# The row maxima of both units of a burst taken in a row, in an attention and mixture-of-experts kernel

## The reference

```python
def xattn(x, context, w_q, w_k, w_v, w_o, b_o):      # 16 heads of 64
    q, k, v = heads(x @ w_q), heads(context @ w_k), heads(context @ w_v)
    attn = softmax(q @ k.T * 64 ** -0.5)
    return merge(attn @ v) @ w_o + b_o

def ffn(x, gate, W1, b1, W2, b2):                    # 8 experts, the best 2 of each token
    raw = softmax(x @ gate)
    w = normalised(top_2(raw))
    return sum_e(w[e] * (relu(x @ W1[e] + b1[e]) @ W2[e] + b2[e]))

x = x + xattn(layernorm(x), ctx, ...)
x = x + ffn(layernorm(x), ...)
```

## Time and profile before

| | |
|---|---|
| median of 3 runs | 1580.39 us (1580.01 to 1581.38) |
| the profiled execution: own time, span | 1580.22 us, 1578.5 us |
| TensorE (PE) busy | 1553.8 us, 98% |
| VectorE (DVE) busy | 1176.1 us, 75% |
| ScalarE (ACT) busy | 1108.0 us, 70% |
| GpSimd (POOL) busy | 818.1 us, 52% |

### The profile page before, as it was taken

One profiled execution on the slowest core, in us unless ns is written; L12 is line 12 of the kernel. 1 busy time (PEld: TensorE's weight loads), 2 busy tenths in 40 slices (PEclk: granted clock), 3 DMA queues, 4 the chain that ended last, 5 costly groups with the idle time before them and its releaser, 6 DMA issues.

```text
span 1578.5 us, 45424 instructions
## 1 busy us (share of the span) xinstructions
PE 1553.8 (98%) x14150; PEld 1454.0 (92%) x14151; DVE 1176.1 (75%) x3796; ACT 1108.0 (70%) x3357; POOL 818.1 (52%) x946
## 2 busy tenths in 40 slices
PE   8999999999999999999999999999999999999997
PEld 7899999999899999999999989998899999999997
DVE  4777777777777777777777777777788777777775
ACT  5677677677776777767767777676666676777774
POOL 2344545545554554554555455455456555555556
PEclk9999999999999999999999999999999999999999
DMA  6522111222111221211122211122799755555554
GB/s 201 145 72 74 60 60 60 77 90 72 62 60 60 67 94 66 74 60 60 63 75 89 74 60 60 60 67 81 241 231 249 144 86 85 89 86 90 84 84 61
DMA packets 105643, 145.05 MB, mean 92 GB/s; under 512 B 12736, under 2 KB 87616, under 8 KB 105344
## 3 DMA queue, kind: packets, MB, share of 16 engines
q1 hardware_dynamic: 60144, 89.00, 17.8%
q0 software_dynamic: 26816, 37.32, 13.7%
q10 hardware_dynamic: 18640, 18.19, 4.4%
HBM read 77.09 MB, written 67.38 MB: 92 GB/s over the span
## 4 chain that ended last, share of the span: by engine, by line
issue 47%; POOL 22%; PE 9%; DVE 7%; DMA 6%; DVEq 3%; ACT 2%; POOLq 2%; ACTq 1%; SPq 0%
POOL lists L662 7%; DMA out<-stage_room,number 6%; PE bank_a L1404 4%; POOL prob L669 3%; DVE hid L1332 3%; POOL rstd L648 2%; DVE stage_room L1349 2%; POOL stage_room L711 2%; POOL stage_room L707 2%; POOL out L735 2%; DVEq L1344 1%; PE bank_v L1437 1%; POOLq L729 1%; PE bank_s L1422 1%; DVEq L1323 1%
## 5 line engine op out<-in xcount | busy, mean ns | idle before, releaser
L669 POOL TENSOR_TENSOR prob<-prob,inv 128x512 f32<-128x512 f32 x256 | 271.4, 1060 | 520.3 <-DVE inv L956 519.6
L777 ACT ACTIVATE prob<-bank_s,low 128x128 f32<-128x128 f32 x1024 | 363.3, 376 | 40.9 <-DVE low L951 40.9
L735 POOL DMA_INDIRECT out<-stage_room,number x142 | 231.8, 1632 | 53.9 <-issue 53.1
L951 DVE TENSOR_REDUCE low<-bank_s 128x4 f32<-128x512 f32 x256 | 175.4, 685 | 98.0 <-PE bank_s L1422 97.9
L777 ACT ACTIVATION_READ_ACCUMULATOR prob<-bank_s,low 128x1 f32 x1024 | 221.1, 216 | 0.0
L770 ACT ACTIVATE probt<-bank_t 128x512 f32<-128x512 f32 x256 | 153.4, 599 | 89.6 <-PE bank_t L1411 89.6
L1050 DVE SCALAR_TENSOR_TENSOR stage_room<-xin,wo_t 128x256 f32<-128x256 f32 x480 | 178.8, 426 | 0.0
L807 ACT ACTIVATE ot_h<-bank_v 128x512 fp32r<-128x512 f32 x128 | 77.4, 604 | 138.4 <-PE bank_v L1437 138.4
L885 ACT ACTIVATE hidt_h<-hid 128x512 fp32r<-128x512 f32 x142 | 89.7, 632 | 117.4 <-DVE hid L1332 112.2
L1411 PE MATMUL bank_t<-ident,prob 128*128 128x128 f32 x1024 | 161.9, 281 | 4.0 <-POOL prob L669 4.0
L1404 PE MATMUL bank_a<-xt_l,wq_h 128*128 128x256 f32 x512 | 152.4, 298 | 0.3 <-DVE xt_l L966 0.3
(11 more groups left out here) (231 smaller groups left out, 4728.9 us busy)
## 6 DMA issues: line engine op xcount, KB each, us to landing
stage_room<-lists ACTq DMA_DIRECT2D x67, 265.0 KB
halves<-stage_room SPq DMA_DIRECT2D x32, 512.0 KB
homes<-halves SPq DMA_DIRECT2D x16, 1024.0 KB, 6.4
xin<-in_x SPq DMA_DIRECT2D x32, 256.0 KB, 2.8
stage_room<-in_x SPq DMA_DIRECT2D x32, 256.0 KB
stage_room<-in_w SPq DMA_DIRECT2D x32, 256.0 KB, 4.3
out<-stage_room SPq DMA_DIRECT2D x32, 256.0 KB, 2.2
cin<-in_ctx SPq DMA_DIRECT2D x32, 128.0 KB, 2.6
```

What stands on the lines that cost most here:

```text
L669: pool.tensor_tensor(prob[:, n % 4, :, :], prob[:, n % 4, :, :], wide(inv[:, n % 4, :], P), ALU.mult).then_inc(s_norm.sem, 1)
L735: pool.indirect_dma_start(out, bass.IndirectOffsetOnAxis(ap=number[:, u, b:b + 1], axis=0), ysum[:, u, b, :], None, compute_op=ALU.add).th ...
L777: e = act.activation(prob[:, n % 4, h, :], bank_s[n % 2][:, h * P:(h + 1) * P], ACT.Exp, bias=low[:, n % 4, h:h + 1], scale=-1.0, accum_ou ...
L951: dve.tensor_reduce(low[:, n % 4, :], bank_s[n % 2][:, :].rearrange("p (h k) -> p h k", h=4), AX.X, ALU.min).then_inc(s_low.sem, 1)
```

## The change

VectorE takes the extremes of both units in the even slot, one right behind the other, and nothing in the odd slot. ScalarE makes the exponentials of u0 and u1 of pass 0 back to back in slot 0; in all other places its order stays.

```diff
--- before.py
+++ after.py
@@ -816,7 +816,11 @@
                             copy_t(it, late, (n - 2) % 8)
                         if n == 6 and has(it, PREV):
                             numerators(it, x1[:, :, D:])
-                        if has(it, CUR):
+                        if isinstance(it, int) and it == 0 and n < 2:
+                            if n == 0:
+                                exps(it, 0)
+                                exps(it, 1)
+                        elif has(it, CUR):
                             exps(it, n)
                         for name, o in A_SLOTS[n]:
                             if (name, o) in HI_EVENTS and has(it, o):
@@ -1122,8 +1126,9 @@
                     for n in range(8):
                         if isinstance(it, int) and (it, n) in WHEN:
                             prepare(*WHEN[it, n])
-                        if has(it, CUR):
+                        if n % 2 == 0 and has(it, CUR):
                             lowest(it, n)
+                            lowest(it, n + 1)
                         if n == 1 and has(it, NEXT):
                             wait(dve, ln1_step, it, "bn1_1")
                         if n == 4 and has(it, PREV):
```

## The result

The changed kernel took **1600.08 us** (median of 4 runs, 1599.09 to 1601.43) against 1580.57 for the kernel before: ratio 1.0123, 95% interval 1.0108 to 1.0138. It is slower by 19.5 us where 4.4 were forecast, and outside the range of 1581.2 to 1587.4.

A forecast was written before the change was run, and what follows sets the result against it. The prediction took TensorE, busy in 98% of the span, to bound the kernel; in the loop it never waits for VectorE or ScalarE. Its terms, 4.4 - 0.6 + 0.6 = +4.4 us, gave 1584.8 us, range 1581.2 to 1587.4.

The forecast's parts named there:

- I take these at nothing: Loop slots other than slot 4's chain: shifts of 0.60 us have room, so no cost; otherwise up to 0.1 us a pass.
- Term 1: Loop, passes 1 to 30: new TensorE wait before k00 for the context's low part, 30 x 0.145 = +4.4 us.
- the edge needs 0.11 and has 0.11: Slot 4: from the low part's end to k00's weight load there is no room, so 0.14 to 0.15 us a pass.
- The lower bound: Loop at k00: 30 x 0.08 = +2.4 us, if the edge needs only 0.05 as that from GpSimd does.
- the wait at k00 swallows that of u3's transposition: Slot 4's chain: u3's transposition, 0.08 us late, need not be counted apart, as a later wait on VectorE's line covers it.
- A larger wait: Rival, loop: u3's transposition over 0.1 us late, or reduction costing 0.69: 0.25 us a pass, +7.5, 1588 us; chance 0.06.
- Term 2: Pass 0: TensorE's second burst 1.22 us sooner, its wait 0.96, then a chain in slot 4 longer by 0.60: -0.6 us.
- the bound of -1.2: Pass 0: the gain in us if the longer chain in slot 4 doesn't bind.
- Term 3: Last pass: TensorE's waits for u3 and u5 come 0.60 later without adding up: +0.6 us, bounds 0 and +1.5.
- The edge has room: Rival, loop at k00: the low part is wanted later or VectorE has slack, loop at zero, 1580.4 us; chance 0.14.
- the ends pay: Rival, pass 0: the whole 2.18 us wait and the lower-clock stretch go, the loop doesn't pay, 1576.5 us; chance 0.06.
- The clock: Rival, loop: new short waits bring TensorE to half its clock once a pass, +28 us, 1613 us; chance 0.02.

The follow-up runs named there:

- B: Session on one chip: one-slot versions of the change against the kernel before, pass 0 only 0.9990, pair in slot 2 only 1.0005, reciprocal between slot 2's reductions 1.0014.
- E: Session on one chip, single executions: changed kernel 1597.79 us; slot 4 paired with transfers 0.6 later 1597.54; changed kernel with fourth transfer moved away 1583.02.
- slot 4 alone: Against the kernel before, VectorE's two reductions paired in slot 4 only, in every pass, ScalarE's order as before: 1582.45 us, ratio 1.0010.
- chip A: Chip of the first measurement and traces, which one was not recorded: changed kernel 1600.08 us against 1580.57 for the kernel before, ratio 1.0123.
- the first burst of pass 0 alone: Against the kernel before, VectorE's and ScalarE's change for u0 and u1 of pass 0 only, all else as before: 1578.53 us, ratio 0.9990.
- F: Session on one chip, single executions: changed kernel 1598.47 us; changed kernel with SyncE's three later issues held until v11 is in its bank 1597.60.
- D: Session on one chip: changed kernel measured again 1583.31 us, ratio 1.0023; slot 4 paired with 640 idle columns zeroed by GpSimd 1583.55, 1.0029.
- four runs without that control: Slot 4 paired with 320 or 640 idle columns zeroed; changed kernel with SyncE's issues held or fourth transfer moved: 1584.37, 1584.72, 1583.88, 1582.21 us.
- C: Session on one chip with two slot-4-paired kernels zeroing idle columns and two edits of the changed kernel: 1584.37, 1584.72, 1583.88, 1582.21 us.

## Why the prediction was right or wrong

**The loop, the step that failed: "I take these at nothing."** That sentence dealt with slot 2, where the reciprocal of u1 moves by 0.60. The check made there was whether u1's own transposition has room, and it has the earlier trace rows. What was not followed is the rest of GpSimd's queue behind that multiplication: four indirect transfers that move with it, the last to the start of slot 4. On chips with the late release that makes the next slot's first reduction 0.47 late, and the prediction's chain was laid from a fixed start, 1.20 behind the burst. The chain itself was right to the hundredth (3.80), its anchor was not. The price per pass went from 0.05 to 0.52 and over 28 passes from 1.5 to 14.7 us.

**Term 1's size.** Where the anchor holds, that is with the first reduction at 1.19, a pass with the pair in slot 4 (chips B to E) is 34.21 to 34.22, 0.05 longer, not 0.145. The step that failed is "the edge needs 0.11 and has 0.11". In the loop it needs 0.05: 629.15 + 0.68 = 629.83 and the weight load at 629.88, in the run with slot 4 alone (burst at 624.17), whose rows are

```profile
629.15 0.68 DVE L1159 TENSOR_TENSOR xt_l<-cin,xt_h 128x512 fp32r<-128x512 f32 x1
```
```profile
629.88 0.19 PEld L1473 LDWEIGHTS bank_a<-xt_l,wk 128*128 128x128 f32 x1
```
```profile
628.06 0.60 PE L1413 MATMUL bank_t<-ident,prob 128*128 128x128 f32 x4
...
629.82 0.28 PE L1406 MATMUL bank_a<-xt_h,wq_h 128*128 128x256 f32 x1
...
630.11 0.28 PE L1474 MATMUL bank_a<-xt_h,wk 128*128 128x256 f32 x1
```

The matmuls stand at 3.89, 5.65 and 5.94 behind the burst, where they were at 3.90, 5.64 and 5.88: nothing is lost at u3's transposition, and the 0.06 comes at k00, as the prediction has it. The 0.11 of the earlier trace rows was measured in pass 0, which is straight code, and taken for the loop. The edge is not the same in both: where k00 waits for the low part it is 0.11 to 0.12 us in pass 0 of the kernel before and in pass 1 of each kernel with the pair in slot 4, and 0.05 in the loop. That is also why pass 1 is 0.12 longer and the others 0.05. What makes the edge shorter in the loop is not shown. The lower bound, 0.08 a pass or 2.4 us, was made with the right 0.05; the measured 0.05 a pass lies below even that, because some 0.03 are made up behind the late weight load. (The range's low end of 1582.4 doesn't follow from that bound, which gives 1580.4 + 2.4 = 1582.8.)

It was also said that the wait at k00 swallows that of u3's transposition. That was right. On chip A TensorE loses 0.40 at u3's transposition, and VectorE's low part, which doesn't depend on it, ends at 634.43 + 0.68 = 635.11; k00's weight load at 635.16 follows it by the 0.05 of the edge, whatever was lost before. The rival *A larger wait* names that transposition, but with 0.25 us a pass.

**Term 2.** The second burst with a wait of 0.96 was forecast; it is 0.97 in the changed kernel, 1.2 us sooner. What is left of it, forecast at -0.6, can't be read from pass 0's length: in four traces of the same changed kernel that pass took 34.96, 35.51, 37.14 and 37.58 us (35.24 before, one trace). The kernel with the first burst of pass 0 alone gives -0.1%, some 1.6 us, near the bound of -1.2 rather than the value taken.

**Term 3.** From the last pass to the end the changed kernel took 4.0 us longer than the kernel before (chip A's trace, 495.16) on chip A, 2.5 on F, 0.3 on E and 0.3 less on D. On D the two waits of TensorE did grow, from 1.73 and 1.18 to 1.99 and 1.71, 0.8 in all where 0.6 were forecast, yet nothing of it is seen in the time to the end. On A they are 2.81 and 1.72, and a copy of ScalarE's is waited for 1.73 where it was 0.68. TensorE's granted clock was at 0.73 and 0.83 for 20 us there; the kernel before has 0.83 for 10 us of this stretch, and E and F, with the same first wait of 2.8, have 0.83 for 10 us too. So the longer time at the lower clock on A doesn't follow from that wait alone, and its cause stays open.

**The whole.** On chip D the kernel is slower by 3.8 us, the forecast was 4.4, and 1583.3 lies in the range; there too the terms differ (loop 2.3 with pass 29's 0.65 in place of 4.4, the rest mostly pass 0). So the nearness owes something to luck. On A, E and F it is 16 to 19.5.

**The other rivals.** *The edge has room* and *the ends pay* are out: the pass with the pair in slot 4 is longer on every chip. But of the 0.11 us at k00's edge in the loop 0.06 were room. *The clock*: 1.00 throughout the loop, in spite of a 0.5 us wait a pass, so the swing that the Trainium skill describes in "TensorE: Matmul & The Clock Gate", section "A second HAM failure mode: psum-queue depth-cycling", doesn't show in the loop. The Trainium skill says in "VectorE: DVE Perf Modes", section "The DRAIN you can't avoid", that the next operation doesn't start until the pipeline of the one before is empty, and adds that one which isn't held starts earlier. The changed kernel repeats what the rows of before said: two reductions of 0.69 us and then the reciprocal take 631.84 - 630.63 = 1.21 us from start to start, 0.60 to 0.61 each.

## What to carry to other kernels

When an instruction moves, follow every queue that it releases to its end, not only to the first consumer with room: here the consumer had 0.5 us of room and the transfers queued behind it did the harm. Room is shared: two delays that cost nothing and 0.05 us by themselves cost 0.52 together, so add up all that enters a chain before comparing it with its slack. And before a mechanism is argued from an experiment, run the changed kernel itself beside it on the same chip; four runs without that control looked like a refutation and were none.

## What the hardware showed that was not expected

*A release that comes late behind an indirect transfer.* In four of the six sessions (A, B, E, F), a wait of ScalarE or VectorE for TensorE that falls due soon after GpSimd starts the fourth, back-to-back indirect transfer ends 1.5 to 1.7 us behind that start, though TensorE's work was done up to 1.4 us before. Seen with the transfer at -0.82, -0.63, -0.04 and, in the last pass, +0.45 (copy or reduction at 0.76, 1.00, 1.53 and 2.00). VectorE's instructions that need no release go on through it (its products start at -0.15, 0.19 and 0.54, on chip A as on D). In two (C, D) it is absent, in D with the same kernel and the same times on GpSimd. The third transfer does not do it: at -1.33 in the changed kernel, with ScalarE's next release on time at -0.92. SyncE's last three issues are not needed. A lock between VectorE and GpSimd alone doesn't explain it: ScalarE is held too, and VectorE's products of two operands, which lie under the same transfer, ran at their usual starts. The Trainium skill ("SBUF — State Buffer", section "SBUF: two separate sides") knows such a lock on a pair of ports that these two engines share, and says that ScalarE never waits on another engine there; by it ScalarE's copy would not have been late, and here it was. What in the machine holds the release, why only the fourth does, and whether it belongs to the chip or to the session stays open; each chip was seen in one session.

*A pass that is longer in every kernel.* In pass 29 GpSimd's fourth transfer started 3.0 to 3.7 us late, with 3.3 to 4.0 us of idle time that nothing in the profile explains (3.51 in the rows above), and the pass took 34.64 to 36.06 us. In the three runs that issue it a slot later the pass had its usual length (34.16, 34.22 and 34.22). Nothing here says why pass 29.
